# Filler matmuls beside an LSTM recurrence on one core: fuller stretches, attention heads moved beside the first steps, gate chunks in pairs

## The reference, cut to what matters

```python
x = x + block(x, cond)     # x (4, 512, 256): hyperbolic attention block, 16 heads of 16, FFN 256 -> 1024 -> 256
x = x + lstm(x, cond)      # LSTM over the 512 time steps, 4 rows of the batch, hidden size 256

xW = einsum('ntd,dk->tnk', x, Wx) + b
def step(carry, xw_t):                 # 512 times, one after the other
    prev_h, prev_c = carry
    a = xw_t + prev_h @ Wh
    i, f, o = sigmoid(a[:, 0:256]), sigmoid(a[:, 256:512]), sigmoid(a[:, 512:768])
    g = tanh(a[:, 768:1024])
    next_c = f * prev_c + i * g
    next_h = o * tanh(next_c)
```

## Time and profile before

| | us |
|---|---|
| median of three runs | 1783.91 |
| lowest, highest | 1780.02, 1800.12 |
| the profiled execution | 1792.91 |
| its span | 1791.2 |
| its granted TensorE clock, mean | 0.801 of 2.4 GHz |

### The profile page before, as it was taken

How to read it: one execution, slowest core, us unless ns; L and a number is a source line. 1 busy time by engine, 2 the same in 40 slices (tenths; PEclk the granted TensorE clock), 3 DMA queues, 4 the chain that set the end, 5 groups by cost and what they waited for, 6 DMA issues and landing times.

```text
span 1791.2 us, 64180 instructions
## 1 busy us (share of the span) xinstructions
PE 1570.5 (88%) x24605; PEld 1269.0 (71%) x24605; DVE 1196.0 (67%) x6690; ACT 933.0 (52%) x3335; POOL 457.9 (26%) x1246
## 2 busy tenths in 40 slices
PE   3656567768799999999999999999999999999998
PEld 3545445446687778787878787877787777878776
DVE  6455567666567767677677777676557666675665
ACT  0333457766446656566566665665344544544433
POOL 4222211121231424142424233232404133140100
PEclk9676665556888867677688887789689999998999
DMA  7000000000000000000000000000000000000000
GB/s 235 0 0 0 0 1 1 1 1 1 5 2 9 3 8 3 8 3 9 3 8 3 9 3 8 3 9 3 8 2 9 9 3 8 3 6 5 3 6 5
DMA packets 16704, 18.29 MB, mean 10 GB/s; under 512 B 6036, under 2 KB 15384, under 8 KB 16408
## 3 DMA queue, kind: packets, MB, share of 16 engines
q1 hardware_dynamic: 13016, 10.51, 2.1%
q10 hardware_dynamic: 3392, 3.81, 0.7%
HBM read 12.21 MB, written 2.10 MB: 8 GB/s over the span
## 4 chain that ended last, share of the span: by engine, by line
PE 58%; DVE 17%; ACT 5%; issue 4%; POOL 2%; DVEq 0%; ACTq 0%; POOLq 0%
PE psum L784 24%; PE psum L828 14%; PE psum L760 4%; PE psum L732 3%; PE psum L725 3%; PE psum L660 3%; DVE weights L1152 2%; DVE cnew L1389 2%; ACT ot L1004 2%; PE psum L774 2%; DVE hl L1398 2%; PE psum L740 2%; DVE hl L1396 2%; DVE gO L1384 2%; POOL sc L464 2%
## 5 line engine op out<-in xcount | busy, mean ns | idle before, releaser
L784 PEld LDWEIGHTS psum<-hl,wh 128*128 128x128 f16 x16384 | 490.7, 98 | 137.4 <-DVE hl L1398 121.4
L784 PE MATMUL psum<-hl,wh 128*128 128x8 f16 x16384 | 520.6, 172 | 27.3 <-DVE hl L1398 8.9
L828 PE MATMUL psum<-zeros,ident 128*128 128x256 f16 x2534 | 388.2, 296 | 5.9
L998 ACT ACTIVATE tA<-gA 128x16 f32<-128x16 f32 x512 | 110.4, 216 | 509.2 <-DVE gA L1380 509.2
L828 PEld LDWEIGHTS psum<-zeros,ident 128*128 128x128 f16 x2534 | 244.2, 105 | 82.4 <-issue 20.1
L1380 DVE TENSOR_REDUCE gA<-psum 128x16 f32<-128x32 f32 x512 | 97.1, 190 | 222.9 <-PE psum L784 217.8
L1152 DVE TENSOR_TENSOR weights<-w,weights 128x256 f16<-128x256 f32 x512 | 201.1, 417 | 17.3 <-ACT weights L901 16.9
L907 ACT ACTIVATE w<-psum 128x512 f32<-128x512 f32 x256 | 154.6, 604 | 27.7 <-DVE weights L1152 26.0
L901 ACT ACTIVATE weights<-psum 128x512 f16<-128x512 f32 x256 | 154.1, 602 | 16.9 <-PE psum L672 16.8
L1396 DVE TENSOR_TENSOR hl<-ot 128x8 f16<-128x8 f32 x512 | 89.8, 175 | 92.4 <-ACT ot L1004 90.7
L1004 ACT ACTIVATE ot<-cnew 128x8 f32<-128x8 f32 x512 | 109.6, 214 | 74.1 <-DVE cnew L1389 14.9
(11 more groups left out here) (301 smaller groups left out, 2412.3 us busy)
## 6 DMA issues: line engine op xcount, KB each, us to landing
arena<-in_x_dram SPq DMA_DIRECT2D x4, 512.0 KB, 9.9
wf<-in_L_cond_w_f_dram SPq DMA_DIRECT2D x2, 1024.0 KB, 17.6
xr<-in_x_dram SPq DMA_DIRECT2D x64, 32.0 KB, 1.8
out_dram<-place SPq DMA_DIRECT2D x64, 32.0 KB, 1.6
qTs<-in_L_cond_w_ada_dram ACTq DMA_DIRECT2D x1, 1536.0 KB
oT<-in_L_cond_Wh_dram ACTq DMA_DIRECT2D x1, 1024.0 KB, 14.5
wx<-in_L_cond_Wx_dram SPq DMA_DIRECT2D x1, 1024.0 KB, 18.1
rows<-in_L_cond_b_ada_dram ACTq DMA_DIRECT2D x4, 128.0 KB, 14.1
```

The source lines that it names most:

```text
L784: last = mm(cols, wh16[:, half, kc, (g0 + c) * P:(g0 + c + 1) * P], hl[:, :, kc, :, 2].rearrange("p e b -> p b e"), start=False, stop=c == ...
L828: mm(pF[:, D:2 * D], ident16[:], zeros[:], start=False, stop=False, skip_group_check=True)
```

## The change

`beside` now returns columns only (scores count 256, a round's 2048 stay), and `keep_busy` fills every stretch up to at least BESIDE = 2750 columns, rounded up to whole fillers, with no limit by time; the stretches t < 4 and, below t = 300, those with t mod 64 of 0 or 1 are filled to RAISE = 4500. Quarter 1's heads go from slots -79..-16 to -19..44, quarter 2's from 19, 21, .. to 46, 48, .. and quarter 3's from 147, 149, .. to 174, 176, .. SETTLE goes from 12 to 13. In `merged_ahead` the two questions to GpSimd stand in r = 3 and r = 5, and their answers are awaited in r = 5 and r = 7; the product that needs them goes from r = 7 to 8. The second of two gate chunks in one slot no longer waits for the copy of the first, and ScalarE waits for both before it copies the first.

```diff
-SETTLE = 12
+SETTLE = 13
-WANTED, FIRST_STEPS = 2900, 4000
+BESIDE, RAISE, HEADS_END = 2750, 4500, 300
...
-    return (FIRST + i, FIRST + B * H + 4 + i, 19 + 2 * i, 147 + 2 * i)[block]
+    return (FIRST + i, -19 + i, 46 + 2 * i, 174 + 2 * i)[block]
...
                 if k < 2 * B:
-                    if r == 2:
+                    if r == 3:
                         powers((num("rh", H), num("smx", H), HALF_DOWN, H))
-                    if r == 4:
+                    if r == 5:
                         powers((one("cbm"), one("cam"), HALF_DOWN, 1))
...
-                        else:
+                        elif GATES_AT[gi - 1] < r:
                             pe.wait_ge(s["n_xc"], GC * n + gi)
...
-                cols, us = 264 * (t - 5 in HEAD_AT) + 512 * (t in HEAD_AT), 0.33 * (t - 5 in HEAD_AT) + 0.45 * (t in HEAD_AT)
+                cols = 264 * (t - 5 in HEAD_AT) + 256 * (t in HEAD_AT) + 256 * (t % RING == 4 and t > RING) + 2048 * ((t + 1) % ROUND == 0)
...
-                count = int(min((WANTED - 256 - cols) / D, (1.3 - us) * 2400 / D))
-                if t < 4:
-                    count = (FIRST_STEPS - 256 - cols) // D
+                wanted = RAISE if t < 4 or t % 64 in (0, 1) and t < HEADS_END else BESIDE
+                count = -((beside(t) - wanted) // D)
...
-                        act.wait_ge(s["n_g"], GC * n + gi + 1)
+                        act.wait_ge(s["n_g"], GC * n + gi + 1 + GATES_AT[gi + 1:].count(r))
...
+            answer = {}
+
+            def ask_for(what, last):
+
+                nonlocal asked
+                asked += 1
+                answer[what] = asked
+                last.then_inc(s["q_in"], 1)
...
-                if r == 2:
+                if r == 3:
...
-                    ask(d.tensor_scalar(num("smx", H), num("ssn", H), 1.0, None, ALU.max))
+                    ask_for(("heads", k), d.tensor_scalar(num("smx", H), num("ssn", H), 1.0, None, ALU.max))
+                if r == 5:
+                    v.wait_ge(s["m_now"], k + 1)
+                    ask_for(("row", k), d.tensor_scalar(one("cam"), one("now"), 1.0 / (HEAD * HEAD), TINY, ALU.mult, ALU.max))
+                    v.wait_ge(s["q_out"], answer[("heads", k)])
                     link(d.tensor_scalar(num("fr", H), num("rh", H), REACH, 1.0, ALU.mult, ALU.min))
                     link(d.tensor_tensor(num("fd", H), num("fr", H), F("rd"), ALU.mult))
-                if r == 4:
-                    v.wait_ge(s["m_now"], k + 1)
-                    ask(d.tensor_scalar(one("cam"), one("now"), 1.0 / (HEAD * HEAD), TINY, ALU.mult, ALU.max))
+                if r == 7:
+                    v.wait_ge(s["q_out"], answer[("row", k)])
                     link(d.tensor_scalar(one("sow"), one("cbm"), REACH, 1.0, ALU.mult, ALU.min))
...
-                if r == 7:
+                if r == 8:
                     v.wait_ge(s["m_F"], k + 1)
```

More of the change, by code:

```diff
@@ L805, in beside @@
             def beside(t):
-                cols, us = 264 * (t - 5 in HEAD_AT) + 512 * (t in HEAD_AT), 0.33 * (t - 5 in HEAD_AT) + 0.45 * (t in HEAD_AT)
-                cols, us = cols + 256 * (t % RING == 4 and t > RING), us + 0.25 * (t % RING == 4 and t > RING)
+                cols = 264 * (t - 5 in HEAD_AT) + 256 * (t in HEAD_AT) + 256 * (t % RING == 4 and t > RING) + 2048 * ((t + 1) % ROUND == 0)
                 for k in range(NT):
-                    cols, us = cols + 256 * (t - merged_slot(k) == SETTLE), us + 0.25 * (t - merged_slot(k) == SETTLE)
+                    cols += 256 * (t - merged_slot(k) == SETTLE)
                 for r in ((t + PAUSE) % RING, (t + PAUSE) % RING + RING):
                     if r < ROW_TILE and 0 <= (t + PAUSE - r) // RING < NT:
[L813 to L817, removed]
+                        cols += 1024 * ((r in (1, 2)) + (38 <= r < 42) + (r in WF1_AT) + WF2_AT.count(r) + GATES_AT.count(r)) + 256 * (r in (25, 56))
+                return cols
             def keep_busy(t):
-                cols, us = beside(t)
-                count = int(min((WANTED - 256 - cols) / D, (1.3 - us) * 2400 / D))
-                if t < 4:
-                    count = (FIRST_STEPS - 256 - cols) // D
+                wanted = RAISE if t < 4 or t % 64 in (0, 1) and t < HEADS_END else BESIDE
+                count = -((beside(t) - wanted) // D)
                 if count > 0:
```

## The result

The changed kernel takes 1705.55 us (median of four runs, 1699.95 to 1708.45). The kernel before takes 1792.01 us over the four runs made of it by then (1780.02 to 1831.31). The ratio is 0.9535, with a 95% interval of 0.9458 to 0.9612: 4.65% faster. The forecast was 1674 us with a range of 1640 to 1722, and faster at 0.94. The sign and the range held; the time came out 31.5 us above the forecast. The profiled execution took 1704.82 us, its span is 1703.1 us.

What follows compares the result with a forecast made beforehand. It took the stretch ahead of step 0 and the half-clock steps as open to the change. Terms -10 - 43 + 8 + 13 - 81 + 6 - 12 = -119 on 1791.2 gave 1672, with 1.7 outside the span 1674 us; range 1640 to 1722.

Steps and rivals of the forecast that it cites:

- -81 us beside heads: Steps 46 to 305: 622 us against 702.9 if the clock holds, at 2.37 us a step plus 5.5 for raised stretches.
- Rival 3: Steps 46 to 305: the clock isn't held, half-clock steps stay and cost more; 1826 us, slower; chance 0.06.
- ahead of step 0: Everything before the first LSTM step: shortened by -10 - 43 + 8, so step 0 starts at 426 us instead of 471.5.
- -43 + 8: Between quarter 0's heads and step 0: 102.1 us becomes 9 + 50; the last 19 slots go from 32 to 40.
- Rival 2: Ahead of step 0: the chain needs its slots whatever is beside it, 76 us for 50; 1700 us; chance 0.12.
- steps 0 to 45: First 46 steps, now with heads in each: 132 us against 118.8, plus 13 (bounds 0 and 45).
- Rival 1: First steps: stalls to 3.5 us or more bring the clock down and fuller stretches keep it low; 1710 us; chance 0.14.
- The GpSimd answer for k = 4 to 7: Steps 0 to 45: late answers' wait costed at nothing; its price otherwise 1 to 3 us a block.
- the gate pair: Slots with two gate chunks: TensorE's 0.94 us idle goes, with the 3.2 us step ahead of the round; ScalarE's wait costs nothing.
- steps 46 to 305: 260 steps with a head every second step: 622 us plus 6 for clock falls, against 702.9.
- The term for falls, 6 us: Steps 46 to 305: the clock is taken to hold but for a fall or two, plus 6 us.
- rival 4: Steps from 46 on: the clock holds, but added fillers are on the path, 0.09 us a step; 1716 us; chance 0.08.

Runs made afterwards that it cites:

- e7: The kernel before with only the new filler rule (2750 columns, 4500 in the raised stretches): 1723.09 us, ratio 0.9695.
- e1: The changed kernel with GpSimd's arithmetic for blocks 8 to 15 moved from r = 2 and 4 to 5 and 7, VectorE's part later too: 1666.24 us, ratio 0.9347.
- e9: e8 with every stretch filled to 2560 columns instead of 2750, one filler less in nearly every stretch: 1684.91 us, ratio 0.9485.
- e8: e1 without the raise to 4500 columns, so 2750 everywhere: 1659.82 us, ratio 0.9344.
- e5: The changed kernel with VectorE again waiting at once for GpSimd's powers in blocks 0 to 7, questions in r = 2 and 4: 1765.18 us, ratio 0.993.
- e4: The changed kernel with each gate chunk waiting again for the copy of the one before, and ScalarE waiting for one chunk only: 1728.13 us, ratio 0.9682.
- e2: The changed kernel with the filler counts of the kernel before, everything else as changed: 1794.0 us, ratio 1.006.

## Why the prediction was right or wrong

**Right: the clock.** The largest term, -81 us beside heads, rested on the half-clock steps going. They do: e7 shows it alone, e1 in full. Rival 3, the slow one, is out. The busy rows could not have told this: TensorE is busy 679.36/702.9 = 97% of the stage at clock 0.78 and 654.17/671.10 = 97% at 0.96 after. Nor could they in two short windows of the kernel before, ten plain steps at the half clock and eleven at the full one:

```profile
1274.00:1306.10 32.10, 31.55 (x420) 24.70 (x419) 16.55 (x107) 9.69 (x48) 11.85 (x42) 0.50 0.01 2
1361.90:1387.50 25.60, 24.96 (x464) 20.10 (x462) 18.38 (x119) 10.55 (x53) 13.40 (x44) 1.00 0.01 4
```

TensorE is busy 98% of the first and 97.5% of the second. e9 and e8, both without the stalls, differ by a filler in each stretch, and e9 falls where e8 does not. The Trainium skill (TensorE: Matmul & The Clock Gate, Part 1, "What's actually happening") ties the clock to how busy the array has recently been; by that rule, the trace agrees between e8 and e9, but the profile's busy row can't stand for it.

**Right: ahead of step 0, by 12 us too cautious.** Quarter 0's heads went from 81.7 to 70.0 us, 11.7 for the 10 forecast, and e5 puts 12.8 us on the split questions. The wait for the answer itself fell by less than the 2.0 us forecast, from 3.1 to 1.6 or 1.7 us for k = 0 to 2. The rest went from 134.1 us (102.1 + 32.0) to 90.3: minus 43.8 for -43 + 8. TensorE begins the scores of slot -19 at 377.9 us. That splits the 9 us between the two: the settling and the chain took 54.6 us for 9 + 50, and the last 19 slots 35.7 for 40. Rival 2 is out. The remaining 2.4 us lie in the first stage, which the change doesn't touch.

**Right: steps 0 to 45.** 128.3 us for 132: four raised steps at 3.3 and 42 at 2.74 on average. The working has a slip, since about 20 x 0.34 and four blocks at 2.2 make 15.6 and not 17.5; with that the sum is 130. Rival 1 did not come, but e4 and e5 show how near it was: one wait of 1.0 or 3.1 us in such a step can bring it on. The GpSimd answer for k = 4 to 7, costed at nothing, cost nothing. VectorE's waits for it in the kernel after:

```profile
DVE sc L1198 <- POOL sc L464: 7.7, 4, 2.8
```

All four belong to k = 0 to 3, ahead of step 0.

**Right: the gate pair, undersized.** 3.24 us became 2.48 at the pair's step, 2.57 in the dense t = 30. But in the forecast a pair was worth the 0.94 us idle and the step ahead of it; e4 says 22.6 us: 14.0 in the fifteen steps themselves, and for the rest the clock that a pair's wait takes along, above all where the moved heads fill every step.

**Wrong: steps 46 to 305.** 671.1 for 628. The step that failed is the one-line treatment of where quarters 2 and 3 go. The prediction checked GpSimd's answers for blocks 4 to 7, and of the rest only block 7's transposes. It didn't follow blocks 8 to 15, whose whole arithmetic runs on GpSimd, into their new slots and past the windows' clip in the same queue. Their collision with the clip is worth 34.8 us here (e1) and, with t = 312, about 5 more in the last stage: 1703.1 - 1213.0 = 490.1 after, 1664.4 - 1179.3 = 485.1 in e1, for 486 forecast. The term for falls, 6 us, assumed a fall or two with no cause; there were seven, each with one.

A smaller miss: 636.3 us in e1 for 622, 14 too much. The last filler took 7.9 where the forecast had 0.02 a step, 5.2, for the fillers (rival 4's mechanism, in nine steps of 32 instead of in all). The raised steps cost 4.4 in this stage (e1 against e8) for 5.5. The rest is the base: with one filler less and no fall the mean is 2.39, for the forecast's 2.35 without its 0.02 for fillers, some 10 us over 260 steps. Most of that sits in the late steps of a window, at 2.6 to 2.8 us each (t mod 32 = 1, 10, 20 and 31), which it also had at 0.02.

Had the pieces not collided, the forecast of 1674 would have stood against e1's 1666, and even there with misses of opposite sign: 11 us too much ahead of step 0, 14 too little beside heads, and 6 for falls that e1 doesn't have. The chances gave no rival this mechanism: what came is 31 us from the forecast, near rivals 1, 2 and 4 in size and none of them in cause. It lies outside the forecast's own 1650 to 1695. That it lies within 1640 to 1722 is luck: that room was meant for other causes.

## What to carry to other kernels

When work is moved in a hand-written schedule, list what follows it on every engine, and lay each of those pieces beside the other periodic work in the same queue; with 16 heads at two slots and windows of 32 slots, a bad phase returns every time. A short wait on the path can cost more than its length: it can take the clock down for several steps (all eight stalls of the kernel after did, and four of the fifteen waits of up to 1 us in e4), so the parts of such a change don't add up: all the rest is worth nothing without the fillers (e2), and with them 18 us as made and 57 with the pieces moved (e7 against after and e1). Hold the clock first, then hunt each wait of 1 us; at the full clock an extra filler costs at most its 0.11 us, and only in steps where TensorE is last (e8 against e9).

## What was unexpected of the hardware

The clock falls with TensorE hardly idle: in e9 it fell at 725.3 us, and 3.26 of the 3.30 us before that were busy. TensorE in e9, t = 114 and 115, both with nine fillers and a head's matmuls:

```profile
722.04 1.01 PE L784 MATMUL psum<-hl,wh 128*128 128x8 f16 x32
722.99 0.39 PE L660 MATMUL psum<-qTs,kT 64*128 64x128 f16 x4
723.31 1.16 PE L822 MATMUL psum<-zeros,ident 128*128 128x256 f16 x9
724.45 1.01 PE L784 MATMUL psum<-hl,wh 128*128 128x8 f16 x32
725.32 0.39 PE L672 MATMUL psum<-vs,weights 128*128 128x33 f16 x8
725.55 2.08 PE L822 MATMUL psum<-zeros,ident 128*128 128x256 f16 x9
```

Nine fillers take 1.16 us at 2.4 GHz and 2.08 in the stretch in which it falls to 1.2 GHz, with no wait ahead of them; t = 115 to 118 take 3.0 to 3.4 us each before it is back. e8, with ten fillers there, had no fall in all its 512 steps. And once it is down, the same stretch is long: t = 120 to 122 in the kernel after, the stall and two half-clock steps behind it, lie in a window of 12.70 us (7.35 us for the same three in e1, from start to start of L1386):

```profile
726.60:739.30 12.70, 0.58 (x3) 0.71 0.01 3
```

And the power of 16 columns on GpSimd takes 2.95 us (L262 above) where one column takes 0.57 us in the same timeline; from step 0 on this power is the longest single instruction of any engine.
